# Dense column tiles between counting groups, copies of x on GpSimd's queue, four banks for the last encoder product, and degrees a few tiles later

## What is computed

```python
x   = layernorm(x + L0(x))     # x: 1250 nodes x 1024, 20000 edges src -> dst
out = layernorm(x + L1(x))

def L0(x):                     # encoder, 3 message layers, decoder
    h = relu(layernorm(x, g, b) @ W1 + b1) @ W2 + b2          # 1024 -> 512 -> 256
    for i in range(3):
        z = h + segment_sum(h[src], dst)
        z = relu(z @ Wa[i] + ba[i]) @ Wb[i] + bb[i]
        h = h + relu(layernorm(z, ng[i], nb[i]))
    return layernorm(x + relu(h @ Wd1 + bd1) @ Wd2 + bd2, out_g, out_b)

def L1(x):                     # two SAGE layers, 1024 wide
    h = relu(x @ Wself0 + mean_of_neighbours(x) @ Wneigh0 + b0)
    return h @ Wself1 + mean_of_neighbours(h) @ Wneigh1 + b1
```

## Time and profile before

| what | us |
|---|---|
| median of 3 runs | 1109.51 (1109.46 to 1112.61) |
| the profiled execution | 1108.93 |
| its span (first to last instruction) | 1107.1 |
| TensorE busy | 1019.6, 92% |
| VectorE busy | 532.7, 48% |
| ScalarE, GpSimd busy | 351.0 and 260.8 |
| granted TensorE clock, mean | 0.959 of full speed |

### The profile page before, as it was taken

The page is one execution under the profiler, slowest core; times in us unless marked ns, Lnnn a source line. Parts: engine busy times, 40 slices in busy tenths (PEclk is TensorE's granted clock), DMA queues, the critical chain, the costliest instruction groups (busy, mean ns, idle before and its releaser), DMA issues.

```text
span 1107.1 us, 14813 instructions
## 1 busy us (share of the span) xinstructions
PE 1019.6 (92%) x4862; PEld 822.2 (74%) x4862; DVE 532.7 (48%) x1314; ACT 351.0 (32%) x632; POOL 260.8 (24%) x314
## 2 busy tenths in 40 slices
PE   4787899798988599899999999999999999999996
PEld 2455668787887478777777777778887777877775
DVE  7968674455747678633222333221334234234545
ACT  5435542233424457622111222111431101222222
POOL 3000000473222533174200706001506102400000
PEclk9688898899998799999999999999999999999998
DMA  5197754299000358431322303332533433202534
GB/s 196 39 208 155 129 142 76 93 206 194 0 21 1 134 199 276 138 118 53 122 98 98 109 0 92 115 136 72 166 108 100 145 117 117 95 1 88 178 122 135
DMA packets 48263, 127.13 MB, mean 115 GB/s; under 512 B 17775, under 2 KB 18784, under 8 KB 48016
## 3 DMA queue, kind: packets, MB, share of 16 engines
q1 hardware_dynamic: 33910, 85.18, 26.3%
q0 software_dynamic: 8000, 27.02, 9.9%
q10 hardware_dynamic: 6298, 14.21, 3.8%
HBM read 101.76 MB, written 45.13 MB: 133 GB/s over the span
## 4 chain that ended last, share of the span: by engine, by line
PE 77%; DVE 8%; ACT 5%; DMA 4%; issue 3%; SPq 1%; POOL 1%; ACTq 0%; DVEq 0%; POOLq 0%
PE bank L1693 40%; PE bank L1714 17%; PE bank L1043 5%; PE bank L1075 4%; PE bank L1400 4%; DMA x_rows<-x 4%; PE bank L613 3%; ACT xt_f L260 1%; DVE stats L380 1%; PE bank L1381 1%; PE bank L1414 1%; DMA w_f<-W_pairs 1%; DVE wide L933 1%; ACT z_new L854 1%; POOL h_f L792 1%
## 5 line engine op out<-in xcount | busy, mean ns | idle before, releaser
L1634 DVE TENSOR_TENSOR h_stage<-h_turned,h_stage 128x1000 fp32r<-128x1000 f32 x80 | 104.0, 1301 | 371.9 <-ACT h_stage L1566 371.9
L1693 PE MATMUL bank<-w_self,h_stage 128*125 128x512 f32 x960 | 230.3, 395 | 0.0
L1693 PE MATMUL bank<-w_neigh,h_stage 128*125 128x512 f32 x960 | 227.0, 396 | 3.4 <-issue 3.4
L1693 PEld LDWEIGHTS bank<-w_neigh,h_stage 128*125 128x125 f32 x960 | 177.9, 186 | 47.4 <-issue 3.6
L1693 PEld LDWEIGHTS bank<-w_self,h_stage 128*125 128x125 f32 x960 | 177.9, 185 | 45.7
L1714 PE MATMUL bank<-g_rows,a_stage 125*125 125x512 f32 x800 | 192.4, 394 | 0.0
L1566 ACT ACTIVATE h_stage<-h_turned 128x1000 fp32r (+1 forms) x80 | 83.8, 1049 | 305.9 <-PE bank L1693 293.4
L1714 PEld LDWEIGHTS bank<-g_rows,a_stage 125*125 125x125 f32 x800 | 148.3, 185 | 37.6
L1531 POOL CAST w_self<-w_stage 128x512 fp32r<-128x512 f32 x32 | 22.7, 709 | 229.3 <-PE bank L1693 221.6
L1075 PE MATMUL bank<-a_turned,gn 125*128 125x418 f32 x360 | 70.5, 354 | 2.9 <-DVE gn L937 2.4
L613 PE MATMUL bank<-xt,w 128*128 128x252 f32 x480 | 63.4, 296 | 8.2 <-ACT xt_f L260 8.2
(11 more groups left out here) (204 smaller groups left out, 1162.8 us busy)
## 6 DMA issues: line engine op xcount, KB each, us to landing
a_stage<-at_dram SPq DMA_DIRECT2D x40, 625.0 KB, 4.0
w_stage<-w_self POOLq DMA_DIRECT2D x32, 256.0 KB, 3.1
at_dram<-a_turned SPq DMA_DIRECT2D x10, 625.0 KB, 9.9
w_stage<-w_neigh POOLq DMA_DIRECT2D x24, 256.0 KB, 2.9
dec_y<-x_bd SPq DMA_DIRECT2D x10, 512.0 KB, 4.2
dec_x<-x_ob SPq DMA_DIRECT2D x10, 512.0 KB, 5.3
x_dram<-h_rows SPq DMA_DIRECT2D x10, 512.0 KB, 3.8
h_dram<-o ACTq DMA_DIRECT2D x20, 256.0 KB
```

The lines of the kernel that those rows point to most:

```text
L1634: dve.tensor_tensor(st[u][:, 1, :, :], ht[:, :, bass.ds(t * NT, NT)], raw(st[u][:, 0, :, :]), ALU.subtract).then_inc(st_ready, 1)
L1693: mm = pe.matmul(out, st[u][:, a, k, :], w[:, b, k * 512:(k + 1) * 512], start=(k == 0 and p == 0), stop=(k == KD - 1 and p == 2))
```

## The change

Five edits, of which the first moves most.

1. `dense(p)` becomes `dense(p, m)`. The column tile m of pair p - 1 now stands ahead of the counting group m of pair p; `turn_norm(p, 1)` stands behind the fourth tile. The last pair's product still stands alone at the end. ScalarE's list is rewritten to match: a pair p starts with `read_counts(p - 1)`, and the `relu`s of p - 1 stand inside pair p. On VectorE `normalizer(p + 1)` stands behind group 0, `norm_low(p, 0)` behind group 2, and `norm_low(p, 1)` behind the last visits.
2. The six copies of x leave SP's queue for GpSimd's, a pair of them ahead of each of the first three `add_eye`.
3. The last encoder product uses four banks (2, 3, 0, 1) and four buffers (`z1_out`: the two `act_out` and two more). Product j waits for the `relu` of j - 4, and the `relu` of j for the split of j - 4.
4. The sum of the degrees moves behind the first two `g_low` of VectorE, its transpose ahead of `g_tile` 4, the maximum's ahead of `g_tile` 8.
5. The register with the maximum degree is kept for the sage block.

```diff
 def dense(p, m):                                   # TensorE, graph block
+    if m == 0:
+        pe.wait_ge(xt_split, 2 * p + 2)
...
         for p in range(PAIRS):
-            if p > 0:
-                turn_norm(p, 1)
             for j in range(GROUP):
                 if p > 0:
+                    if j < KH:
+                        dense(p - 1, j)
+                    if j == KH - 1:
+                        turn_norm(p, 1)
                     pe.wait_ge(counts_out, GROUP * (2 * p - 1) + j + 1)
...
             if p + 1 < PAIRS:
                 turn_norm(p + 1, 0)
-            dense(p)
+        for m in range(KH):
+            dense(PAIRS - 1, m)
```

```diff
         affine(0, 0)                               # ScalarE, graph block
...
+        affine(0, 1)
+        take_root(1)
+        normalize(1, 0)
+        normalize(1, 1)
+        w1_high(KD // 2)
+        for p in range(1, PAIRS):
+            read_counts(p - 1)
+            if p + 1 < PAIRS:
+                take_root(p + 1)
+            affine(p, 0)
+            relu(p - 1, 0)
+            relu(p - 1, 1)
+            if p + 1 < PAIRS:
+                normalize(p + 1, 0)
+            relu(p - 1, 2)
+            relu(p - 1, 3)
+            z1_high(p - 1)
+            affine(p, 1)
+            if p + 1 < PAIRS:
+                normalize(p + 1, 1)
```

```diff
-            own = slice(p * CH, min((p + 1) * CH, N + 128 - NT))      # SP
-            for to in ("x_bd", "x_ob") if p < NCH else ():
-                sp.dma_start(io[to][own, :], io["x"][own, :]).then_inc(s.x_copied, 16)
...
         for p in range(PAIRS):                                        # GpSimd
+            own = slice(p * CH, min((p + 1) * CH, N + 128 - NT))
+            for to in ("x_bd", "x_ob") if p < NCH else ():
+                pool.dma_start(io[to][own, :], io["x"][own, :]).then_inc(s.x_copied, 16)
             add_eye(p)
```

```diff
+        def z1_relu(j):                            # ScalarE, encoder block
+            act.wait_ge(z_mm, ZD + j + 1)
...
+            if j >= 4:
+                act.wait_ge(z_split, ZD + j - 1)
+            act.activation(z1_out[j % 4][:, :], ps_z1[j % 4][:, 0:CH], ACT.Relu,
...
             for m in range(KH):                    # TensorE, last_dense
                 j = KH * c + m
-                pe.wait_ge(z_split, ZD + j + 1)
-                mm = dense(ps_z[j % 2][:, 0:CH], ...
+                if j >= 2:
+                    pe.wait_ge(z_out, ZD + j - 3)
+                mm = dense(ps_z1[j % 4][:, 0:CH], ...
```

More of the change, by code:

```diff
@@ L286, in relu, with z1_high @@
                            bias=s.biases[:, m:m + 1]).then_inc(z1_relu, 1)
+        def z1_high(p):
+            act.wait_ge(z1_relu, KH * (p + 1))
+            if p == 0:
+                act.wait_ge(w_ready, KD // 2 + 1)
+                act.wait_ge(tab_ready, 1)
+            for h, t in tile_halves(p):
+                hi = act.activation(s.wide[:, 0, :, t * NT:(t + 1) * NT], z1_f32[:, :, h * NE:h * NE + NT], ACT.Copy)
+            hi.then_inc(z1_hi, 1)
         act.dma_start(s.ident[:, :], io["ident"]).then_inc(table_in, 16)
@@ L300, in _ @@
             w1_high(n)
[L301 removed]
+        affine(0, 1)
[15 more added lines that the diff above has]
+            z1_high(p - 1)
             affine(p, 1)
[L303 to L305 removed]
             if p + 1 < PAIRS:
                 normalize(p + 1, 1)
[L308 to L327 removed]
+        read_counts(PAIRS - 1)
+        for m in range(KH):
+            relu(PAIRS - 1, m)
+        z1_high(PAIRS - 1)
     @block.gpsimd
@@ L538, in _ @@
                     if j == 3:
+                        norm_low(0, 1)
                         normalizer(1)
+                else:
+                    if j == 0 and p + 1 < PAIRS:
+                        normalizer(p + 1)
+                    if j == 2:
+                        norm_low(p, 0)
             if p == 0:
@@ L555, in _ @@
                 z1_low(p - 1)
-            if p + 2 < PAIRS:
-                normalizer(p + 2)
         z1_low(PAIRS - 1)
@@ L599, in more, with dense @@
                 mm.then_inc(more_free, 1)
-        def dense(p):
-            pe.wait_ge(xt_split, 2 * p + 2)
-            if p == 0:
-                pe.wait_ge(w_ready, KD // 2)
-            own = slice(p % 2, p % 2 + 2)
-            for m in range(KH):
-                if m == 3:
-                    pe.wait_ge(z1_relu, KH * p + 1)
-                if m in (1, 2) and p + 1 < PAIRS:
-                    pe.wait_ge(xt_affine, KD * (2 * p + 2) + 4 * m)
-                for k in range(KD):
-                    for q, (a, b) in enumerate(HALVES):
-                        mm = pe.matmul(ps_z1[m][:, 0:2 * NE], w1[:, a, k, m * 128:(m + 1) * 128],
-                                       xt[:, own, b, k, :], start=(k == 0 and q == 0), stop=(k == KD - 1 and q == 2))
-                mm.then_inc(z1_mm, 1)
+        def dense(p, m):
+            if m == 0:
+                pe.wait_ge(xt_split, 2 * p + 2)
+                if p == 0:
+                    pe.wait_ge(w_ready, KD // 2)
+            own = slice(p % 2, p % 2 + 2)
+            if m == 3:
+                pe.wait_ge(z1_relu, KH * p + 1)
+            if m in (1, 2) and p + 1 < PAIRS:
+                pe.wait_ge(xt_affine, KD * (2 * p + 2) + 4 * m)
+            for k in range(KD):
+                for q, (a, b) in enumerate(HALVES):
+                    mm = pe.matmul(ps_z1[m][:, 0:2 * NE], w1[:, a, k, m * 128:(m + 1) * 128],
+                                   xt[:, own, b, k, :], start=(k == 0 and q == 0), stop=(k == KD - 1 and q == 2))
+            mm.then_inc(z1_mm, 1)
         pe.sem_inc(more_free, 1)
@@ L923, in _ @@
                 wd2_high((j - KH) // 2)
[L924 removed]
+            z1_relu(j)
     @block.vector
@@ L1012, in split_wide @@
             hi, lo = [s.wide[:, hl, k, c * CH:(c + 1) * CH] for hl in range(2)]
-            split(ZD + j, hi, lo, act_out[j % 2][:, :])
+            split(ZD + j, hi, lo, z1_out[j % 4][:, :])
         dve.sem_inc(z_split, 2)
@@ L1167, in _ @@
             if t == 4:
+                pe.wait_ge(deg_summed, 1)
+                pe.transpose(ps_t[1][0:NT, 0:T], degrees[0:T, :], s.ident[0:T, 0:T]).then_inc(deg_turned, 1)
+            if t == 8:
                 pe.wait_ge(degree_part, 1)
```

79 lines of the change are left out of this document (30 added, 49 removed).

## The result

| what | before | after |
|---|---|---|
| median, us | 1110.89 (1109.46 to 1112.61, 4 runs) | 1073.47 (1072.67 to 1078.98, 4 runs) |
| the profiled execution, us | 1108.93 | 1074.08 |
| its span, us | 1107.1 | 1072.3 |
| TensorE's granted clock, mean | 0.959 | 0.975 |

The ratio is 0.967, with a 95% interval of 0.9652 to 0.9688: 34.7 to 38.7 us faster. The forecast was 1065.3, with a range of 1055 to 1080. The sign and most of the mechanisms were right; the gain was 44.2 on paper and came out at 37.4 by the medians.

What follows compares the result with a forecast made beforehand. TensorE and VectorE take turns as the graph block's bound. Gains of 23.8 (graph block), 4.3 (degrees) and 16.1 (last encoder product), 44.2 in all, bring the median from 1109.5 to 1065.3 us, range 1055 to 1080.

Steps and rivals of the forecast that it cites:

- the ring wait: Graph block: VectorE's 16.1 us of waiting for a place in the ring go, falling to under 3.
- Row waits: Graph block: VectorE's waiting for row loads falls from 11.4 to 4.5 us, bounds 3 and 11.4.
- The round trip in `more`: Graph block, loop more: 3 us of new waiting because TensorE reaches its picks about 2 us behind VectorE; bounds 0 to 8.
- Half clock behind the stops: Graph block: 1.5 us added for counts and tiles at half clock behind the two row waits.
- the rival of the late rows: Graph block: loads wait for whole pieces of the copies; gain 13 instead of 23.8, kernel 1076; chance 0.14.
- the outcome of the late copies: Graph block: GpSimd issues copies only in row waits, costing 4.2 us in each of two pairs; 1074; chance 0.05.
- the prediction's own bound: Graph block: with row waits of 11.4 and half clock behind them as now, it ends at 174, gain 13.
- The low end (2): Degrees: gain 2 us, not 4.3, if the clock falls in the 1.9 us gap.
- the four splits ahead of the first low part: Last encoder product: VectorE's four splits run to 357.7, its first low part to 358.3.
- The hold-up: Last encoder product: four GpSimd instructions delay VectorE about 2 us each, 8; as rival, gain 11 or less, chance 0.10.
- a sign of being wrong: Whole kernel: wrong if visits stop at row loads over 10 us, clock under 0.8 from 48, or decoder or sage lengthen.
- Half clock on the other side: Graph block: TensorE's cut-up work falls to half clock; block ends at 228, 41 us later, kernel 1130; chance 0.04.

Runs made afterwards that it cites:

- the edit that took it away: Changed kernel with VectorE's norm_low(p, 0) and z1_low(p - 1) moved directly ahead of the loop more: 1070.83 us, ratio 0.9663.
- the kernel with Wd2 on VectorE: Changed kernel with the four low parts of Wd2 made by VectorE between its splits, no longer by GpSimd: 1073.39 us, ratio 0.9672.
- With the late copies: Changed kernel with the second and third pair of copies of x moved behind GpSimd's third add_eye: 1069.61 us, ratio 0.9664.
- The early normalize alone: Changed kernel with ScalarE's normalize(p + 1, 1) ahead of affine(p, 1), not behind it: 1072.65 us, ratio 0.9691.
- both edits together: Changed kernel with later copies of x behind GpSimd's third add_eye and normalize(p + 1, 1) ahead of affine(p, 1): 1068.65 us, ratio 0.9625.

## Why the prediction was right, point by point

**Bounds and graph block.** Right: two engines that take turns, the ring wait gone (16.1 to nothing), the rows' wait halved (11.4 to 6.1), the last product alone at the end. The dense block ended at 168.0, not 163.4: a gain of 19.2 in place of 23.8. Three terms were too small. Row waits: 4.5, measured 6.1. The round trip in `more`: 3.0, measured 6.1 (bounds 0 to 8). Half clock behind the stops: 1.5; the two tiles behind them took 4.92 and 4.08 in place of 3.2, 2.6 together, and the counts beside them ran slow too. These add 1.6 + 3.1 + 1.1 = 5.8 to my sum, of which 4.6 reached the end. The largest miss is the round trip, but the edit that took it away made the block only 1.5 us shorter, so it isn't simply added. The step that failed in its reasoning is the row wait. I wrote that the copies should be nearly through when the late load goes out. They left GpSimd at 63.2 and not near 61, because `add_eye(0)` ahead of them waits for the store of the counts:

```profile
62.14 1.14 POOL L338 TENSOR_TENSOR a_turned<-a_turned,ident 125x125 f32 x2 [49.16 <-DMA at_dram<-a_turned]
63.22 0.51 POOL L374 DMA_DIRECT2D x_bd<-x  x1
```

They landed 7.9 and 12.5 us later, the second at 76, beside the load of 70.7. I had put no time on the copies themselves: issued at 61, the second would by these 12.5 us still have landed past 73 (an estimate). That is the rival of the late rows in a small size (7.0 us to landing), and the outcome of the late copies, for another reason than the one given. Each copy took 0.51 us to issue among the visits. The first packets move within 2 us of it, while VectorE is busy throughout (columns as in the earlier trace rows):

```profile
63.00:64.00 1.00, 1.00 (x11) 1.00 (x10) 1.00 (x5) 0.00 (x0) 1.00 (x3) 1.00 0.00 0
64.00:65.00 1.00, 1.00 (x11) 0.88 (x10) 1.00 (x7) 0.85 (x2) 0.24 (x1) 1.00 2.30 749
```

So nothing here shows GpSimd held off by VectorE: of the rule of the Trainium skill, DMA: Bandwidth & Descriptors, section SWDGE vs HWDGE vs iDMA, this trace has no sign. The other rule of the Trainium skill, same page, section Queues, rings and completion order, I read too kindly. Turns go by the packet, and the DMA views above show what a turn of the copies carries: of all packets from 67 to 79, 48 are over 8 KB, and GpSimd's queue moved 2.57 MB, so they carry 53.5 KB each, a whole row piece of the copy. From 70 to 78 it is 0.86 MB, 16 such packets, one for each DMA engine if they are spread evenly. The load beside one of them per engine took 3.4 us longer than alone, beside three 7.1 us. That fits the whole pieces that the rival of the late rows spoke of.

**The move of the copies.** This is the part that I credited wrongly. I took the rows' wait off as the gain of edit 2 in the new order. The runs show the new order alone brings it from 11.4 to about 5 with the copies on SP. The sum counted it once, so the total wasn't wrong by it, but the credit was: edit 2 brought nothing here, and by the graph blocks (117.7 against 119.1 and 120.3) it cost some 2 us. By the prediction's own bound, row waits of 11.4 as before, the block with the copies left on SP would have ended at 174; it ended at 165.7. That the wrong credit did no harm to the total is luck.

**Degrees.** 4.2 us in this trace, forecast 4.3. The low end (2) came in three other executions with the same gap (27.0, 27.0 and 26.8 us of stretch).

**Last product.** Start of the decoder's first product: forecast 17.4 closer, measured 15.3. The step that was off is the four splits ahead of the first low part, which I put at 4.0 together: beside GpSimd's additions to `h_f` they took 5.5, so the second column chunk started 11.2 us after the first and not 9.8; and its eight tiles took 10.8, not 10.1. VectorE's first decoder tile, counted from the first message product: forecast 16.1 closer, measured 13.4 (356.09 - 193.31 against 392.65 - 216.48). The hold-up was put at 8 us and was 10: the three long instructions took 9.3 us in place of 1.3, beside three low parts and the two memsets, which I had not counted; and the four low parts of h's last update (`h_low`) beside the first low part of Wd2 took 3.57 in place of 1.40 (the kernel with Wd2 on VectorE).

**Decoder.** It lengthened from 67.6 to 71.1 us, which I had named as a sign of being wrong. Of the 3.5, 1.9 are no loss of their own: TensorE starts 15.3 us earlier and VectorE's tile 13.4 (the forecast had 17.4 and 16.1). For the rest the prediction had nothing, and 1.5 us went. VectorE's tiles follow each other tightly, and `turn(0)` needs the second of them. TensorE now stands 2.67 us ahead of it, and the transposes and the product behind run slow:

```profile
367.42 1.93 PE L1412 MATMUL bank<-ident,h_rows 125*128 125x125 f32 x8 [2.67 <-ACT h_rows L1317]
369.00 6.53 PE L1431 MATMUL bank<-w_self,wide 128*125 128x512 f32 x24
```

With the late copies the same place went otherwise, and the decoder took 68.2 us in place of 71.1:

```profile
346.17 2.56 DVE L958 CAST wide<-z_out 128x418 fp32r<-128x418 f32 x1
...
348.50 2.27 POOL L1281 MEMSET h_rows<- 128x1024 f32 x2
...
364.72 1.07 PE L1413 MATMUL bank<-ident,h_rows 125*128 125x125 f32 x8 [1.28 <-ACT h_rows L1318]
365.55 5.76 PE L1432 MATMUL bank<-w_self,wide 128*125 128x512 f32 x24
```

The edit touches nothing here. VectorE's cast got in ahead of GpSimd's memsets (2.56, not 4.41 us), TensorE's gap became 1.28, and the clock stayed up: 1.85 us on VectorE became 2.9 at the end. The early normalize alone shows the same, and both edits together the slow way again (2.66 us of gap, 71.0). The cast took 4.40 to 4.41 us in each of the six executions with the gap of 2.7 and 2.56 in both with 1.28. So who comes first here is a race, and I take it for a part of the spread between executions of one kernel; the decoder of one kernel traced in both ways is not among the runs. The medians of such edits can't be read closer than it.

**Register.** No gap at either place, as forecast; no run tested it alone.

**Half clock on the other side.** It did not come: 0.94 was granted in the graph block against 0.88. One sum there was off: a block that ends at 228 and not at 163 costs 65 us for the whole stage, not 75, so the kernel would have been slower from a share of about 0.7.

**The other signs.** The first message product started at 193.3 (forecast 188.5), the decoder's first product at 347.2 (near 340), both by what the graph block and the last product fell short. Row loads landed in 3.7 to 13.1 us, where I had 3.4 to 8: the one of 13.1 went out at 90.1 beside the third pair of copies, and nobody waited for it.

## What to carry to other kernels

Two edits that remove the same wait don't add up: measure each with and without the other before keeping both. A move that takes away one wait can make another of the same size. Where a transfer is moved to another queue, ask what the instruction ahead of it there waits for, since that sets when it collides. And price each new short stop of TensorE with the work behind it at half clock, as one of two outcomes.

## What the hardware showed that I had not expected

- A stop of 1.9 to 2.2 us ahead of the degrees' transpose left the 24 matmuls behind it at 3.1 us in six executions and 4.4 to 4.6 in three, one kernel among both; ahead of the decoder's first transposes the clock stayed up after 1.28 us (two executions) and fell after 2.7 us (all six).
- A load of 512 KB took 3.6 us alone, 7.0 beside 0.86 MB of GpSimd's copies and 10.7 beside 2.57 MB, in packets of 53.5 KB.
- GpSimd's instructions hold up VectorE's splits (0.37 and 0.59 us become 2.2 to 4.4). The Trainium skill, SBUF — State Buffer, section SBUF: two separate sides, has this as an exclusive lock for a whole instruction; the kernel without GpSimd's low parts agrees, and a cast of 4.41 us across a low part and two memsets fits with the next GpSimd instruction taking the lock first.
